# A graph attention kernel on one core: entry loads cut in 112 and 13 partitions, a product table split around the first two transpositions

## What is computed

```python
def _hop(emb, head, tail, rel_e, W, N):
    a_input = jnp.concatenate([emb[head], emb[tail]], axis=-1)
    e = jnp.sum(a_input @ W * rel_e, axis=-1)
    e = jax.nn.leaky_relu(e, NEG_SLOPE)
    seg_max = jax.ops.segment_max(e, head, num_segments=N)
    ex = jnp.exp(e - seg_max[head])
    denom = jax.ops.segment_sum(ex, head, num_segments=N)
    alpha = ex / denom[head]
    agg = jax.ops.segment_sum(emb[tail] * alpha[:, None], head, num_segments=N)
    return agg + emb
# head, tail = src, dst; rel_e = relation_emb[edge_type], 64 types
for _ in range(2):
    emb = _hop(emb, head, tail, rel_e, W, N)
    emb = emb / jnp.maximum(jnp.linalg.norm(emb, axis=-1, keepdims=True), 1e-12)
    res = 0.5 * res + emb
return _layernorm(x + res, axis=-1)
```

## Time and profile before

| | us |
|---|---|
| median of three runs | 5607.83 |
| the profiled execution: time | 5606.45 |
| the profiled execution: span | 5604.7 |
| DVE busy, share of the span | 4144.9, 74% |
| PE busy | 3015.4, 54% |
| ACT busy | 1353.1, 24% |
| GpSimd busy | 3351.9, 60% |

### The profile page before, as it was taken

One profiled execution on the slowest core, in us unless ns is written; L12 is line 12 of the kernel. 1 busy time (PEld: TensorE's weight loads), 2 busy tenths in 40 slices (PEclk: granted clock), 3 DMA queues, 4 the chain that ended last, 5 costly groups with the idle time before them and its releaser, 6 DMA issues. The chain is left out here.

```text
span 5604.7 us, 102618 instructions
## 1 busy us (share of the span) xinstructions
PE 3015.4 (54%) x23517; PEld 2365.8 (42%) x23525; DVE 4144.9 (74%) x14407; ACT 1353.1 (24%) x4964; POOL 3351.9 (60%) x3535
## 2 busy tenths in 40 slices
PE   4411101566656665656666676666666665666662
PEld 1211101454545454445454445554445454454441
DVE  8799997777776777677767657777677767776777
ACT  3322222121212121212121342121212121212125
POOL 0000002777777777777777357777777777777770
PEclk9855555776777777777777667677777777777675
DMA  2000001222222222222222432222222222222223
GB/s 64 0 0 0 0 0 53 59 51 55 53 57 51 54 54 58 51 54 54 55 54 54 79 79 55 55 54 56 53 55 54 55 54 54 54 55 54 55 50 70
DMA packets 260830, 276.45 MB, mean 49 GB/s; under 512 B 166797, under 2 KB 175213, under 8 KB 260454
## 3 DMA queue, kind: packets, MB, share of 16 engines
q0 software_dynamic: 112640, 115.57, 10.5%
q1 hardware_dynamic: 147814, 157.55, 9.4%
HBM read 256.78 MB, written 16.09 MB: 49 GB/s over the span
## 5 line engine op out<-in xcount | busy, mean ns | idle before, releaser
L702 POOL DMA_INDIRECT G<-rows,ixs x3448 | 3270.6, 949 | 1072.0 <-issue 1017.0
L872 DVE SCALAR_TENSOR_TENSOR acc<-acc,aS,psY 65x128 f32 x3520 | 1206.2, 343 | 818.8 <-PE psY L766 560.2
L717 PE MATMUL psX<-PT,oht 128*128 x3532 | 945.9, 268 | 1183.3 <-DVE logit L831 1039.6
L766 PE MATMUL psY<-G,wr 128*65 128x128 f32 x7040 | 1298.9, 316 | 178.0 <-DVE acc L872 155.1
L831 DVE CUSTOM_DVE_ANT_0 junk<-psX,G 128x192 f32<-128x192 f32 x3520 | 1157.1, 346 | 219.4 <-DMA G<-rows,ixs 175.9
L717 PEld LDWEIGHTS psX<-PT,oht 128*128 128x128 bf16 x3532 | 410.0, 116 | 1473.6 <-issue 1458.7
L766 PEld LDWEIGHTS psY<-G,wr 128*65 128x65 f32 x7040 | 906.0, 164 | 268.9 <-issue 231.2
L720 PE MATMUL psX<-v2lo,oht 128*128 128x128 bf16 x3532 | 956.8, 271 | 0.0
L719 PE MATMUL psX<-v,oht 128*128 128x128 bf16 x3532 | 955.1, 270 | 0.0
L718 PE MATMUL psX<-PTlo,oht 128*128 x3532 | 934.2, 264 | 0.0
L795 ACT ACTIVATE wr<-G,wS 128x64 f32<-128x64 f32 x3520 | 862.9, 334 | 0.0
(11 more groups left out here) (175 smaller groups left out, 2530.4 us busy)
## 6 DMA issues: line engine op xcount, KB each, us to landing
tb<-types_lin SPq DMA_DIRECT2D x222, 512.0 KB
G<-rows,ixs POOLq DMA_INDIRECT x3520, 2.4
G<-rows SPq DMA_DIRECT2D x28, 224.0 KB, 4.6
res<-rows SPq DMA_DIRECT2D x28, 224.0 KB, 4.8
mt<-marks_d SPq DMA_DIRECT2D x110, 48.1 KB
rows<-G SPq DMA_DIRECT2D x2, 1568.0 KB, 12.4
rows<-G SPq DMA_DIRECT2D x14, 224.0 KB, 3.3
rows<-res SPq DMA_DIRECT2D x14, 224.0 KB, 4.2
```

Of the source, the lines that this page charges most:

```text
L702: nc.gpsimd.indirect_dma_start(G[:, p, u, L:L + D], None, tab[hop], bass.IndirectOffsetOnAxis(ap=ixs[:, p, u:u + 1], axis=0)).then_inc(gat ...
L717: nc.tensor.matmul(x[:, 0:L], piece, PT[:, bass.ds(first, L)], start=True, stop=False)
L766: nc.tensor.matmul(psY[:, v % 8, :], wr[:, v // 16, v % 16, :], G[:, pq, v, 0:L], start=True, stop=True).then_inc(y_ok, 1)
L872: nc.vector.scalar_tensor_tensor(spot, spot, aS[:, pq, v:v + 1], psY[:, v % 8, :], ALU.mult, ALU.add).then_inc(acc_ok, 1)
```

## The change

- Each load of the edges is cut in two, 112 and 13 partitions. The heads get a semaphore of their own, `heads_in`; DVE's key instruction waits for that, and the payload instruction for `edges`, now the tails and types.
- PE and ACT run 17 lots, then passes 0 and 1, then the last 8 lots, then the other passes.
- The copies to `held` in level 8 behind pass 1, which were ACT's, are DVE's own (`away` only once three passes have been taken).

The diff, cut to its core, in the order SP, PE, DVE, ACT; QB is 25:

```diff
+            QA = 17
...
-                sp.dma_start(hraw[0:RP, 0:RC], src.rearrange("(p c) -> p c", c=RC)).then_inc(edges, 16)
-                sp.dma_start(traw[0:RP, 0:RC], dst.rearrange("(p c) -> p c", c=RC)).then_inc(edges, 16)
-                sp.dma_start(yraw[0:RP, 0:RC], etype.rearrange("(p c) -> p c", c=RC)).then_inc(edges, 16)
+                for raw_t, given, there in ((hraw, src, heads_in), (traw, dst, edges), (yraw, etype, edges)):
+                    rows = given.rearrange("(p c) -> p c", c=RC)
+                    for p0, p1 in ((0, 112), (112, RP)):
+                        sp.dma_start(raw_t[p0:p1, 0:RC], rows[p0:p1, :]).then_inc(there, 16)
...
+                for q in range(QA):
+                    lot(q)
+                pe.wait_ge(prep, 1)
+                for n in range(2):
+                    passed(n)
+                for q in range(QA, QB):
+                    lot(q)
+                for n in range(2, PASSES):
+                    passed(n)
...
-                dve.wait_ge(edges, 48)
+                dve.wait_ge(heads_in, 32)
                 k0 = keys[0][:, :, :].rearrange("p b c -> p (b c)").bitcast(u16)
                 nc.vector.tensor_scalar(k0, hraw[:, :], float(N), float(KOFF), ALU.min, ALU.add)
+                dve.wait_ge(edges, 64)
...
-                    compare(pairs, rest, (0, 1), state["pass"] > 0)
+                    compare(pairs, rest, (0, 1), state["pass"] > 2)
...
-                for level in range(8, 19):
+                for _ in range(2):
+                    passed()
+                for q in range(QA, QB):
+                    lot(q)
+                for level in range(9, 19):
```

## The result

The changed kernel takes **5592.71 us** (median of 13 runs, 5587.8 to 5595.29) against 5607.56 us before (13 runs beside them): 14.85 us less, a ratio of 0.9974 with a 95% interval of 0.9967 to 0.9982. Forecast were 5591.6 us and 16.2 us less. Its profiled execution has a span of 5591.0 us, against 5604.7.

The account below looks back on a forecast made before the run. DVE's standstill ahead of the hops was taken as the bound. 14.25 (entry) + 25.77 (pass 0) − 23.8 (pass 2) = 16.2 us gained, giving 5591.6 us; range 5580 to 5597.

Parts of the forecast that it names:

- Entry: Edge loads at the start: on all 16 DMA engines the payload starts at 17.8 instead of 32.06 us, gaining 14.25.
- x: Load of x behind the edges: in by some 29 to 35 us, against 43.4 before.
- PE's wait ahead of pass 0: After 17 lots PE would wait 12 to 25 us for DVE to hand over its first half.
- Pass 0: First transposition: with 17 lots ahead DVE goes on at 191.69 instead of 217.46 (old time scale), gaining 25.77 us.
- Pass 2: The 8 lots behind pass 1 delay it: DVE goes on at 284.1 instead of 260.35, losing 23.8 us.
- The held copies: Level 8 copies moved to DVE: free while DVE waits for the lots (the cover), 3.7 us if the lots were hidden.
- The hops unchanged: Behind pass 2 nothing is moved, so the hops shift as a whole and keep their length.
- The rival of the clock: Lots behind pass 1 run at PE's upper clock: 40.5 instead of 52.7 us, loss 11.5, time 5579.3; 13%.
- The rival that the loads gain nothing: Cut entry loads keep the edges until 31 us; only 2 us gained, time 5605.8; 8%.
- The slower rival: Lots behind pass 1 lose their pace: at 11 us a lot the loss is 55 us, time 5623; 4%.
- The granted clock: PE's clock column reads 1.00, but by durations of transpositions the lots were taken to run at the lower level.

Follow-up runs that it names:

- e6_xlate: Changed kernel with the issue of x held until the edges are in; one run, sort's end 912.65 us, 15.2 earlier than before.
- e2_split: Changed kernel with the entry loads and single wait of before, so the 17/8 split and held copies alone; 1.1 us less than before, ratio 0.9989 to 1.0008.
- e4_14: Changed kernel with 14 lots ahead of pass 0 and 11 behind pass 1; 7.9 us more than before, ratio 1.0004 to 1.0023.
- e3_20: Changed kernel with 20 lots ahead of pass 0 and 5 behind pass 1; 32.2 us less than before, 33.9 in a second run.
- e10_warm17: Changed kernel (17/8 lots) with extra fp32 transpositions of a block of x on PE in every lot; 5580.56 us against 5606.61 before.
- e7_124: Changed kernel with the entry loads cut at 124 and 1 partitions instead of 112 and 13; one run, sort's end 933.46 us, 5.6 later than before.
- e8_warm32b: Kernel before with the cut entry loads, all 25 lots ahead, and extra fp32 transpositions of x in PE's waits; 5570.05 us against 5606.61.
- e9_onewait: Changed kernel with one wait for all six entry loads ahead of the keys instruction; one run, sort's end 914.22 us, 13.6 earlier than before.

## Why the prediction was right, step by step

- **Entry, forecast 14.25, measured 32.06 − 19.11 = 12.95 us.** The keys came at 16.80 as forecast; the payload came 1.3 us late, because I took 368 GB/s, the store's rate, for 16 engines. The loads ran at 223 to 313 GB/s, also with x held back (e6_xlate), nearer to the other row that I named, 217 to 247. The gain lay inside the bounds (11.5). Why they ran no faster is open. It is not that loads are slow: in the kernel before, a later load with rows of 7,040 bytes (`firstb`, which copies one such row to 128 partitions) moved 396 GB/s from 933.0 to 934.5 us, gathers beside it included. Nor does the rate grow in proportion to the engines: 119 to 137 GB/s on five are some 25 each, 223 to 313 on sixteen 14 to 20 each.
- **x, forecast to be in by 29 to 35 us,** came at 33.6.
- **PE's wait ahead of pass 0, forecast 12 to 25 us,** was 23.45.
- **Pass 0, forecast 25.77:** DVE's comparison moved from 217.46 to 178.72, 38.74 in all; less the entry's 12.95, 25.79.
- **Pass 2, forecast a loss of 23.8:** 260.35 − 244.72 = 15.63 are left of 38.74, a loss of 23.11. Two small errors offset each other: pass 1 ended about 0.5 us later than assumed, since its last transpositions ran slow as well, and the first lot behind it took 195.04 − 189.30 = 5.74 instead of 6.91 us. The second was luck: in e2_split and e4_14 that lot took 6.9 us. e2_split shows the loss without the loads, e4_14 that it grows and e3_20 that it goes with three lots.
- **The held copies, nothing under cover, 3.7 us without:** in e3_20 the cover is gone. From pass 1's first comparison to pass 2's it takes 224.49 − 187.85 = 36.64 us. Before, with the row below, it took 260.35 − 226.35 = 34.00. So 2.6 us, not 3.7: behind a whole copy of 0.62 us the minimum starts after 0.53, and in the kernel before the predicated move came 0.1 us later behind the minimum, since ACT's copy (0.94 us) ended only just ahead of it.

```profile
226.35 0.42 DVE L350 TENSOR_TENSOR swap<-keys 128x512 uint16<-128x512 bf16 x1 [0.35 <-DVE pay L373]
```

- **The hops unchanged:** the sort's end moved by 14.97 of the 15.63, the time by 14.85. The 0.66 between pass 2 and the sort's end are many small steps between 380 and 890 us, whose cause stays open.
- **The rival of the clock** did not happen in the changed kernel beyond its first lot, as the prediction held more likely. Its price was near: made true in e10_warm17, it gave 26.1 us less than before, where the prediction had 28.5 (5607.8 − 5579.3); 1.3 us of the difference are the entry's.
- **The rival that the loads gain nothing** is answered by e7_124: a cut that brings no more engines made the payload 8 us later than before, so the gain is not the cut's but the 112's. The Trainium skill's advice against cutting a transfer (DMA: Bandwidth & Descriptors, section Rules for kernel authors) agrees with e7_124; the gain with 112 and 13 is a case outside it. The busy share until x begins is 2 tenths for 124 partitions, 3 for 125 and 9 for 112. The Trainium skill's rule on divisors (DMA: Bandwidth & Descriptors, section Why a DMA increments its semaphore by 16 and not by 1) gives 4, 5 and 16 engines of 16, which agrees each time. The count of small packets fits too, if every engine that takes part in a load writes one: 3 × (16 + 13 − 5) = 72 more after than before, and as many as before in e7_124 (4 + 1 = 5). The first 100 us of before, after and e7_124:

```profile
DMA packets 16442, 9.03 MB, mean 90 GB/s; under 512 B 12961, under 2 KB 16065, under 8 KB 16440
DMA packets 16514, 9.03 MB, mean 90 GB/s; under 512 B 13033, under 2 KB 16137, under 8 KB 16512
DMA packets 16441, 9.02 MB, mean 90 GB/s; under 512 B 12961, under 2 KB 16065, under 8 KB 16440
```

- **The slower rival:** no lot ahead of pass 0 or behind pass 1 took clearly more than 6.9 us; but a split three lots further the wrong way was enough to make it slower (e4_14), by the forecast's own mechanism.

The granted clock was read rightly from the durations. In the changed kernel's windows around the first lot behind pass 1 the clock column falls, and the pair of matmuls takes 1.12 us at 1.00 and 2.07 at 0.50 (2.4 and 1.2 GHz):

```profile
191.03 1.12 PE L289 MATMUL psP<-eT,wqp 64*128 64x512 f32 x2 [0.67 <-ACT eT L535]
...
196.77 2.07 PE L289 MATMUL psP<-eT,wqp 64*128 64x512 f32 x2 [0.67 <-ACT eT L535]
```

```profile
193.00:194.00 1.00, 0.22 (x1) 0.00 (x0) 1.00 (x3) 0.73 (x2) 0.00 (x0) 1.00 0.00 0
194.00:195.00 1.00, 0.52 (x1) 0.12 (x1) 1.00 (x2) 0.43 (x1) 0.00 (x0) 0.56 0.00 0
195.00:196.00 1.00, 1.00 (x5) 0.54 (x4) 1.00 (x3) 0.58 (x1) 0.00 (x0) 0.50 0.00 0
```

The 17 lots ahead of pass 0 have 2.07 us too, so they ran at 0.50, although the column reads 1.00 for all of the first 190 us.

## What to carry to other kernels

When work on a shared in-order engine is moved from ahead of a handover to behind the next one, price both gaps with the same unit: here 6.9 us a lot, 23 us idle ahead of pass 0, 29 us behind pass 1. Split where the first gap is just full (20 of 25 lots: 32 to 34 us less than before; 17: 15 less; 14: 8 more). Before splitting at all, see whether the work can be made short enough to fit where it was: with its matmuls at the upper clock all 25 lots fitted, for 36.6 us.

## What the runs showed of the hardware that I had not expected

- Filler of 16 bf16 transpositions of an identity for each lot left the matmuls at 2.07 us to the end; 11 fp32 transpositions of a block of x brought them to 1.12 within three lots (two in e10_warm17). The two fillers differ in type, in data, in number and in how long they keep PE busy (87% and 98% of the time at 2.07 us); which of these counts was not tried.
- Once the matmuls with fp32 filler took 1.12 us, they did so for all remaining lots of e8_warm32b, with PE busy 37.34 of 50 us; without filler the clock fell back within one lot (the windows above). The window among the lots of e8_warm32b:

```profile
100.00:150.00 50.00, 37.34 (x189) 18.68 (x187) 49.93 (x59) 28.55 (x50) 0.00 (x0) 1.00 0.00 0
```

- Whether the first lot behind pass 1 starts at the upper level changes from kernel to kernel: its pair of matmuls took 1.12 us in the changed kernel, e3_20, e6_xlate and e7_124, and 2.07 in e2_split, e4_14 and e9_onewait. No run says what decides it. It is worth 1.2 us.
- On 16 engines the loads of 6,800-byte rows ran at 223 to 313 GB/s, little above those of 256-byte rows (214 to 242). The store of 1,540-byte rows had 368, the gathers of some 26 GB/s beside it included, and the load of one 7,040-byte row to all partitions 396. What makes the difference was not tried.
- The span behind the sort's end took 4676 to 4678 us in eight of the profiled executions (before and after among them) and 4683 to 4687 in the other six, e3_20 both times. No run says why. Differences of a few us between two times of whole kernels are therefore not told apart from it; the sort's end is the safer mark.
